# Orders of blocks 0 and 1 in a fused MLP with per-sample experts: x of block 2, the drain of block 0, and the loads of x of block 0

## The chip, the core and the metric

The kernel runs on one core of a Trainium2 chip. The metric is the device time of one execution in microseconds (us); the time of a kernel is the median of its runs.

## The reference

```python
def ref(x, indices, fc1_w, fc1_b, fc2_w, fc2_b, experts_w, experts_b):
    h = gelu(einsum('bnd,hd->bnh', x, fc1_w) + fc1_b)            # exact gelu
    shared = einsum('bnh,sh->bns', h, fc2_w) + fc2_b
    expert_x = einsum('bnh,bph->bnp', h, experts_w[indices]) + experts_b[indices][:, None, :]
    return concatenate([shared, expert_x], axis=-1)
out = x + ref(x, itok, fc1_w, fc1_b, fc2_w, fc2_b, experts_w, experts_b)
```

All is float32. x is 32 x 256 x 256; the hidden size is 1024; fc2_w gives 192 of the 256 outputs, and one of 16 experts, picked for each of the 32 rows of x, gives the other 64.

## The kernel before, in words

The work goes in 16 blocks (`BLOCKS`) of two rows of x, 512 tokens each. Every float32 operand of a matmul is split in a high half (rounded, by ScalarE) and a low half (the rest, by VectorE or GpSimd, which is called POOL below), and each product is made of three: high x high, high x low, low x high. fc1 of a block gives eight chunks of 128 hidden units; two chunks are a *pair*. ScalarE applies the gelu and makes the high half of a pair, then the low half is made, and `fc2_units` on TensorE (PE) multiplies pair and fc2 weights into the two accumulators of the block (`acc_ps`, one for each row of x). A *drain* on VectorE adds an accumulator to `resid`, which by then holds x plus bias (`residual` on POOL), and SyncE (SP) stores it.

Blocks 0 and 1 (`PLAIN`) make fc1 in the plain way, `conv_chunk(0)` to `conv_chunk(15)`. Blocks 2 to 15 use Strassen's scheme with seven products (`product`), which needs sums of quarters of w1 (S1 to S4, indices 0 to 3, made in the order `S_ORDER` = 0, 1, 3, 2) and of x (T1 to T4, `t_sum`). A block from 2 on is made in two groups, t = 0 for the first group of block 2. Its products stand between `fc2_units` of the block before.

Operands must lie transposed. x of block 0 and w1 are transposed by PE (`x0_bank`, `w1_bank`), everything else in two steps: a DMA brings pieces of 32 partitions, and VectorE transposes 32 x 32 squares into PSUM (`w2_square`, `experts_square`, `x_square`, `s_square`), from where ScalarE takes the high half (`..._high`) and VectorE the low half (`..._low`).

The order on each engine is written out by hand; the engines meet only at semaphores. An engine works strictly in its own order, so a step that waits holds everything behind it. What matters for the change:

- SP's queue issues the loads: x of block 0 (`load_x(0)`, one load of 512 KB, L263), the second half of w1 (L235), w2 (L286), experts 0 (L251), pieces of x of block 1 (L268), experts 1, w1's pieces for the S sums (`load_w1_pieces`, L279), pieces of x of block 2, the bias of fc2 (L294), x of block 1, and so on. The first half of w1 is issued by ScalarE's queue.
- PE starts with `warm` matmuls (L921), the transposes of x of block 0 (L915), ten more warm matmuls, the transposes of w1's first half, `first_chunk` (L954), the transposes of w1's second half, chunks 1 to 7 (L947), then `fc2_units` of block 0 between chunks 8 to 15 of block 1. Chunk c waits for the gelu of chunk c - 4. `fc2_units(0, ...)` waits for the low half of its pair, for w2 and for the experts; chunk 8 waits for `x1_low`.
- Block 2 on PE: the product with A11, then `fc2_units(1, 0)`, which waits for `plain_low(4)`, for expert half 0 of block 1 and for the drain of block 0 (`drained`, L803 to L810). The product with S1 waits for `xt_lo` (`x_sums_lo`) and for all four `s_low`.
- VectorE makes, between `x1_low` and the loop over blocks from 2 on: expert halves 0 and 1 of block 1 (L692, L700), the four S squares and lows (`s_square` L656, `s_low` L662), x of block 2 (L711, L715, L752, L757), the low halves of pairs 4 to 7 (`plain_low`, L720) and the drains of block 0 (L805, L807, L810).
- ScalarE makes the gelus (L513), the high halves of pairs (`conv_high`, L501), `s_high` (L425), `experts_high` (L441), `b_copy` (L475), `x_high` (L461, L464) and `x_sums_high` (L491).
- POOL makes the low halves of pairs 0 to 3 (L344), the four weight sums (L366), `residual(0)` (L337), `x_sums_lo` of block 2 (L352), `residual(1)`.

## Time and profile before

| | us |
|---|---|
| median of 3 runs | 374.62 (374.12 to 375.15) |
| the profiled execution | 375.64 |
| its span | 373.9 |
| PE busy in it | 360.3 (96%) |
| VectorE, ScalarE, POOL busy | 223.9 (60%), 243.2 (65%), 221.7 (59%) |
| HBM read, written | 28.97 MB, 8.39 MB |

The profile is of one execution. All times of rows are counted from the start of its span; 1.74 us of the execution lie outside of it. In the names of rows, numbers are left out: `fc_ps` is fc1_ps, `w_in` is w1_in (which also takes the S sums), `w_piece` is w1_piece or w2_piece, `b` is b1 or b1_in. "idle before" is the time in which the engine had nothing to do just before a row, with what ended it.

### The profile page before, as it was taken

Reading aid. Unit: us, or ns where it says so; the run is one execution under the profiler, and the core shown is the slowest. Engines: PE = TensorE matmul, PEld = TensorE weight load, DVE = VectorE, ACT = ScalarE, POOL = GpSimd, SP = SyncE. Lnnn points to the kernel's source line nnn. Section 1 sums busy time; section 2 is a strip of 40 time slices with the busy share of each in tenths; the row PEclk is TensorE's granted clock in tenths of the full one; section 3 lists DMA queues with packets and bytes.
Section 4 is the critical chain, followed back from the end, with each engine's and each line's share of the span. In section 5 each row is a group of like instructions: output and inputs, shape, how many; then the busy total and the mean of one; then the engine's idle time right before and its main releaser. Section 6 shows DMA issues by size and latency. Waiting matters only on the chain.

```text
span 373.9 us, 7841 instructions
## 1 busy us (share of the span) xinstructions
PE 360.3 (96%) x2863; PEld 353.4 (95%) x2863; DVE 223.9 (60%) x367; ACT 243.2 (65%) x410; POOL 221.7 (59%) x100
## 2 busy tenths in 40 slices
PE   6999939999999999999999999999999999999996
PEld 4788939999999999999999999999999999999996
DVE  1583788394765839386683938567393856744341
ACT  2495536675785957577594857769485767947560
POOL 0059440477666666766666677656667775666381
PEclk9899978999999999999999999999999999999999
DMA  8979844326160432516133252605135230403011
GB/s 193 187 156 108 160 107 120 86 68 166 41 177 27 131 94 87 149 53 161 48 113 95 89 146 64 169 30 149 57 93 142 64 114 31 125 23 114 2 56 56
DMA packets 70431, 37.86 MB, mean 101 GB/s; under 512 B 43514, under 2 KB 70394, under 8 KB 70394
## 3 DMA queue, kind: packets, MB, share of 16 engines
q1 hardware_dynamic: 69776, 36.85, 39.4%
q10 hardware_dynamic: 618, 0.53, 0.7%
q8 instruction: 22, 0.36, 0.4%
q14 instruction: 15, 0.12, 0.1%
HBM read 28.97 MB, written 8.39 MB: 100 GB/s over the span
## 4 chain that ended last, share of the span: by engine, by line
PE 81%; issue 3%; DVE 3%; ACT 2%; POOL 1%; DVEq 0%; POOLq 0%
PE fc_ps L971 36%; PE acc_ps L1003 15%; PE acc_ps L1005 15%; PE acc_ps L1007 15%; POOL ht L344 1%; ACT ht L501 1%; DVE ht L720 1%; DVE w1t L662 1%; DVE work L715 0%; ACT gelu L513 0%; ACT gelu L527 0%; DVE tr_ps L656 0%; DVE tr_ps L711 0%; DVE work L785 0%; DVE resid L810 0%
## 5 line engine op out<-in xcount | busy, mean ns | idle before, releaser
L344 POOL TENSOR_TENSOR ht<-gelu,ht 128x1024 fp32r<-128x1024 f32 x60 | 144.2, 2404 | 124.5 <-ACT ht L501 124.5
L971 PE MATMUL fc_ps<-xt,w1t 128*128 128x256 f32 x1176 | 173.9, 284 | 0.0
L971 PEld LDWEIGHTS fc_ps<-xt,w1t 128*128 128x128 f32 x1176 | 155.8, 193 | 0.6 <-ACT gelu L513 0.3
L1003 PE MATMUL acc_ps<-w2t,ht 128*128 128x256 f32 x512 | 145.8, 285 | 5.8 <-DVE resid L807 5.7
L1005 PE MATMUL acc_ps<-w2t,ht 128*128 128x256 f32 x512 | 145.5, 284 | 0.0
L1007 PE MATMUL acc_ps<-w2t,ht 128*128 128x256 f32 x512 | 145.5, 284 | 0.0
L1003 PEld LDWEIGHTS acc_ps<-w2t,ht 128*128 128x128 f32 x512 | 99.0, 193 | 6.5 <-issue 5.8
L1005 PEld LDWEIGHTS acc_ps<-w2t,ht 128*128 128x128 f32 x512 | 99.0, 193 | 0.3
L1007 PEld LDWEIGHTS acc_ps<-w2t,ht 128*128 128x128 f32 x512 | 99.0, 193 | 0.0
L501 ACT ACTIVATE ht<-gelu 128x1024 fp32r<-128x1024 f32 x64 | 67.8, 1063 | 3.3
L487 ACT ACTIVATE work<-fc_ps 128x512 f32<-128x512 f32 x28 | 16.8, 599 | 57.4 <-PE fc_ps L971 57.4
L769 DVE TENSOR_TENSOR work<-fc_ps,work 128x512 f32<-128x512 f32 x28 | 19.3, 691 | 54.6 <-PE fc_ps L971 45.8
L352 POOL TENSOR_TENSOR xt<-work,xt 128x1024 fp32r<-128x1024 f32 x14 | 33.6, 2403 | 17.9 <-ACT xt L491 17.9
L337 POOL TENSOR_TENSOR resid<-resid,bias 128x1024 f32<-128x1024 f32 x16 | 38.7, 2416 | 0.9 <-DMA bias<-in_L_cond_fc_b 0.9
L778 DVE TENSOR_TENSOR work<-fc_ps,work 128x512 f32<-128x512 f32 x28 | 19.2, 686 | 32.0 <-PE fc_ps L971 32.0
L441 ACT ACTIVATE w2t<-tr_ps 128x512 fp32r<-128x512 f32 x32 | 18.7, 590 | 29.0 <-PE acc_ps L1007 29.0
L527 ACT ACTIVATE gelu<-work,b 128x512 f32<-128x512 f32 x56 | 37.1, 712 | 0.7 <-DVE work L785 0.7
L785 DVE TENSOR_TENSOR work<-fc_ps,work 128x512 f32<-128x512 f32 x28 | 19.4, 692 | 12.9 <-PE fc_ps L971 11.2
L539 ACT ACTIVATE gelu<-work,b 128x256 f32<-128x256 f32 x56 | 25.2, 501 | 0.0
L700 DVE TENSOR_TENSOR w2t<-tr_ps,w2t 128x512 fp32r<-128x512 f32 x32 | 22.1, 692 | 4.7 <-ACT w2t L441 3.1
L793 DVE TENSOR_TENSOR work<-fc_ps,work 128x512 f32<-128x512 f32 x28 | 19.1, 684 | 7.2 <-PE fc_ps L971 7.2
L544 ACT ACTIVATE gelu<-fc_ps,b 128x256 f32<-128x256 f32 x56 | 23.2, 469 | 0.0
(57 smaller groups left out, 281.7 us busy)
## 6 DMA issues: line engine op xcount, KB each, us to landing
resid<-in_x SPq DMA_DIRECT2D x16, 512.0 KB, 4.0
pieces<-in_L_cond_experts_w SPq DMA_DIRECT2D x128, 64.0 KB, 1.9
out<-resid SPq DMA_DIRECT2D x32, 256.0 KB, 2.7
pieces<-in_x SPq DMA_DIRECT2D x60, 128.0 KB, 3.7
bias<-in_L_cond_experts_b SPq DMA_DIRECT2D x32, 32.0 KB, 2.9
w_piece<-in_L_cond_fc_w SPq DMA_DIRECT2D x4, 256.0 KB, 4.6
w_piece<-in_L_cond_fc_w SPq DMA_DIRECT2D x4, 192.0 KB, 8.1
w_in<-in_L_cond_fc_w SPq DMA_DIRECT2D x4, 128.0 KB, 5.8
```

The lines of the kernel that those rows point to most:

```text
L337: nc.gpsimd.tensor_tensor(rows, rows, bias[:, par, :, :].unsqueeze(2).to_broadcast([P, R, T, OUT]), ALU.add).then_inc(resid_ready, 1)
L344: nc.gpsimd.tensor_tensor(ht[:, slot, LO, :, :].rearrange("p k t -> p (k t)"), gelu[:, q % GELUS, :, :].rearrange("p k t -> p (k t)"), ht[ ...
L352: nc.gpsimd.tensor_tensor(xt[:, n % 2, X_T1:X_T4 + 1, LO, :], t_sum, xt[:, n % 2, X_T1:X_T4 + 1, HI, :].bitcast(FP32), ALU.subtract).then_ ...
L501: nc.scalar.activation(ht[:, q % PAIRS, HI, :, :].rearrange("p k t -> p (k t)"), gelu[:, q % GELUS, :, :].rearrange("p k t -> p (k t)"), A ...
L527: nc.scalar.activation(gelu[:, q % GELUS, j, :], upper[:, j, :], ACT.Gelu, bias=b1[:, k:k + 1]).then_inc(up_gelu, 1)
L539: nc.scalar.activation(gelu[:, q % GELUS, j, SEQ:2 * SEQ], c22[:, j, :], ACT.Gelu, bias=b1[:, k:k + 1]).then_inc(c22_gelu, 1)
L544: nc.scalar.activation(gelu[:, q % GELUS, j, 0:SEQ], fc1_ps[:, BANK_A[t % 2], j * SEQ:(j + 1) * SEQ], ACT.Gelu, bias=b1[:, k:k + 1]).then_ ...
L700: nc.vector.tensor_tensor(expert_columns(LO, ks), tr_ps[:, half, :].rearrange("p (k b c) -> p b k c", k=HALF, b=R), expert_columns(HI, ks) ...
L971: last = nc.tensor.matmul(fc1_ps[:, dst, j * SEQ:(j + 1) * SEQ], w1t[:, w, wv, ms], xt[:, n % 2, o, xv, :], start=(fresh and j == 0 and at ...
L1003: nc.tensor.matmul(dst, h_hi_t, w_hi, start=(r == 0 and u % (2 * T) == 0), stop=True, skip_group_check=True)
L1005: nc.tensor.matmul(dst, h_hi_t, w_lo, start=False, stop=True, skip_group_check=True)
L1007: last = nc.tensor.matmul(dst, h_lo_t, w_hi, start=False, stop=True, skip_group_check=True)
```

## The change

Loads of x of block 0: two loads of 256 KB, each with a semaphore of its own, in place of one; SP waits for the first of them before it issues the second half of w1 and all that follows. PE transposes each half of x when it is there. The pieces of x of block 2 are issued ahead of experts 1 and w1's pieces. VectorE and ScalarE take the second half of w1 ahead of w2. On VectorE x of block 2 goes ahead of expert half 0 of block 1 and of the S steps, the drains of block 0 go behind the last S step and ahead of `plain_low(6)`; ScalarE follows with `b_copy`, `x_high`, `x_sums_high` and the S steps; POOL makes `x_sums_lo` of block 2 ahead of the weight sums.

```diff
@@ -112,6 +112,7 @@
                     for n in range(PLAIN)]
         xt0 = xt_plain[0]
 
+        x0_loaded = [sem(f"x0_loaded{b}") for b in range(R)]
         x_loaded = [sem(f"x_loaded{n}") for n in range(2)]
         xp_loaded = [sem(f"xp_loaded{n}") for n in range(2)]
         e_loaded = [sem(f"e_loaded{n}") for n in range(2)]
@@ -280,7 +281,11 @@
                                  .rearrange("p q k j -> p (q k) j"), w1_pieces[q])\
                         .then_inc(w1p_loaded, 16)
 
-            load_x(0)
+            for b in range(R):
+                ts = slice(b * T, (b + 1) * T)
+                sp.dma_start(resid[:, 0, ts, :], x_blocks[0][:, ts, :]).then_inc(x0_loaded[b], 16)
+
+            sp.wait_ge(x0_loaded[0], 16)
             load_w1(sp, 1)
             for q in range(Q):
                 sp.dma_start(w2_piece[S * q:S * (q + 1), :, :], w2_v[q]).then_inc(w2_loaded, 16)
@@ -288,9 +293,9 @@
             numbers = load_experts(0)
             load_x_pieces(1)
             load_expert_bias(0, numbers)
+            load_x_pieces(2)
             numbers = load_experts(1)
             load_w1_pieces()
-            load_x_pieces(2)
             sp.dma_start(
                 bias[:, :, :, 0:SHARED].rearrange("p a b o -> p (a b) o"),
                 fc2_b.rearrange("(o c n) -> o c n", o=1, c=1).to_broadcast([P, 2 * R, SHARED]))\
@@ -331,7 +336,11 @@
         def _(pool):
             def residual(n):
                 par = n % 2
-                pool.wait_ge(x_loaded[par], 16 * (n // 2 + 1))
+                if n == 0:
+                    for b in range(R):
+                        pool.wait_ge(x0_loaded[b], 16)
+                else:
+                    pool.wait_ge(x_loaded[par], 16 * ((n + 1) // 2))
                 pool.wait_ge(be_loaded[par], 16 * R * (n // 2 + 1))
                 rows = resid[:, par, :, :].rearrange("p (b t) d -> p b t d", b=R)
                 nc.gpsimd.tensor_tensor(
@@ -373,6 +382,7 @@
 
             for r in range(PAIRS):
                 pair_lo(r)
+            x_sums_lo(PLAIN)
             pool.wait_ge(w1p_loaded, 16 * Q)
 
             pool.wait_ge(w1_tr, 2 * D)
@@ -386,7 +396,6 @@
 
             pool.wait_ge(x0_tr, D)
             residual(0)
-            x_sums_lo(PLAIN)
             residual(1)
             for n in range(PLAIN, BLOCKS):
                 for g in range(GROUPS):
@@ -566,9 +575,9 @@
             act.wait_ge(b1_ready, 1)
             conv_chunk(0)
             w1_high(1, 0)
+            w1_high(1, 1)
+            conv_chunk(1)
             w2_high(0)
-            conv_chunk(1)
-            w1_high(1, 1)
             w2_high(1)
             conv_chunk(2)
             w2_high(2)
@@ -585,24 +594,24 @@
                 x1_high(d)
             conv_chunk(7)
             conv_high(2)
+            b_copy(PLAIN)
+            x_high(PLAIN)
+
+            conv_chunk(8)
             conv_high(3)
-
-            conv_chunk(8)
+            x_sums_high(PLAIN)
             conv_chunk(9)
             conv_high(4)
             experts_high(1, 0)
             s_high(0)
             conv_chunk(10)
-            b_copy(PLAIN)
-            x_high(PLAIN)
             conv_chunk(11)
             conv_high(5)
+            s_high(1)
+            s_high(3)
             conv_chunk(12)
-            x_sums_high(PLAIN)
-            s_high(1)
             conv_chunk(13)
             conv_high(6)
-            s_high(3)
             s_high(2)
             conv_chunk(14)
             conv_chunk(15)
@@ -815,12 +824,12 @@
                 w1_low(0, d)
             dve.wait_ge(b1_tr, 1)
             nc.vector.tensor_copy(b1[:, :], fc1_ps[:, 3, 0:K]).then_inc(b1_ready, 1)
+            for d in range(D):
+                w1_low(1, d)
             w2_square(0)
             w2_square(1)
-            w1_low(1, 0)
             w2_low(0)
             w2_square(2)
-            w1_low(1, 1)
             w2_low(1)
             w2_square(3)
             w2_low(2)
@@ -837,33 +846,33 @@
                 x1_low(d)
 
             dve.wait_ge(x1_lo, D)
-            experts_square(1, 0)
-            s_square(0)
-            plain_low(4)
-            experts_low(1, 0)
-            s_low(0)
-            dve.wait_ge(e_lo, 3)
-            dve.wait_ge(s_lo, 1)
             for d in range(D):
                 x_square(PLAIN, d)
-            plain_low(5)
             x_sums_first(PLAIN)
             x_low(PLAIN, 0)
             x_sums_last(PLAIN)
             x_low(PLAIN, 1)
             dve.wait_ge(xb_lo, 2)
             dve.wait_ge(t_added, 4)
+            experts_square(1, 0)
+            plain_low(4)
+            s_square(0)
+            experts_low(1, 0)
+            s_low(0)
+            dve.wait_ge(e_lo, 3)
+            dve.wait_ge(s_lo, 1)
             s_square(1)
             s_square(3)
-            plain_low(6)
+            plain_low(5)
             s_low(1)
             s_low(3)
-            drain(0, 0)
-            drain(0, 1)
             dve.wait_ge(s_lo, 3)
             s_square(2)
             experts_square(1, 1)
             s_low(2)
+            drain(0, 0)
+            drain(0, 1)
+            plain_low(6)
             plain_low(7)
 
             for n in range(PLAIN, BLOCKS):
@@ -921,9 +930,14 @@
                     nc.tensor.matmul(fc1_ps[:, 2, 0:2 * P], bits[:, 0:P], bits,
                                      start=True, stop=True)
 
-            def x0_bank(d):
-                transposes(tr_ps[:, d, :], [feature_chunk(resid[:, 0, t, :], d)
-                                            for t in range(TILES)]).then_inc(x0_tr, 1)
+            def x0_banks(b):
+                pe.wait_ge(x0_loaded[b], 16)
+                for d in range(D):
+                    last = transposes(tr_ps[:, d, b * SEQ:(b + 1) * SEQ],
+                                      [feature_chunk(resid[:, 0, b * T + t, :], d)
+                                       for t in range(T)])
+                    if b == R - 1:
+                        last.then_inc(x0_tr, 1)
 
             def w1_bank(half, d):
                 transposes((acc_ps, tr_ps)[half][:, d, :], [
@@ -1013,9 +1027,8 @@
 
             pe.wait_ge(ident_ready, 1)
             warm(WARM)
-            pe.wait_ge(x_loaded[0], 16)
-            for d in range(D):
-                x0_bank(d)
+            for b in range(R):
+                x0_banks(b)
             warm(WARM // 2)
             pe.wait_ge(w1_loaded[0], 16 * Q)
             for d in range(D):
```

VectorE, from the squares of x of block 2 or the S squares up to `plain_low(7)` and what follows it. First the kernel before (L656 is `s_square`, L662 `s_low`, L720 `plain_low`, L805 to L810 the drains, L692 an expert square):

```order
L656 STREAM_TRANSPOSE tr_ps<-w1_in 128x512 x2
L720 TENSOR_TENSOR ht<-gelu,ht 128x1024
L662 TENSOR_TENSOR w1t<-tr_ps,w1t 128x512 x2
L805 TENSOR_TENSOR resid<-acc_ps,resid 128x2x192
L807 TENSOR_TENSOR resid<-acc_ps,resid 128x2x64
L810 TENSOR_TENSOR resid<-acc_ps,resid 128x512
L656 STREAM_TRANSPOSE tr_ps<-w1_in 128x512
L692 STREAM_TRANSPOSE tr_ps<-pieces 128x4x4x32
L662 TENSOR_TENSOR w1t<-tr_ps,w1t 128x512
L720 TENSOR_TENSOR ht<-gelu,ht 128x1024
```

The changed kernel at the same place (L665 is `s_square`, L671 `s_low`, L729 `plain_low`, L814 to L819 the drains):

```order
L665 STREAM_TRANSPOSE tr_ps<-w1_in 128x512 x2
L729 TENSOR_TENSOR ht<-gelu,ht 128x1024
L671 TENSOR_TENSOR w1t<-tr_ps,w1t 128x512 x2
L665 STREAM_TRANSPOSE tr_ps<-w1_in 128x512
L701 STREAM_TRANSPOSE tr_ps<-pieces 128x4x4x32
L671 TENSOR_TENSOR w1t<-tr_ps,w1t 128x512
L814 TENSOR_TENSOR resid<-acc_ps,resid 128x2x192
L816 TENSOR_TENSOR resid<-acc_ps,resid 128x2x64
L819 TENSOR_TENSOR resid<-acc_ps,resid 128x512
L729 TENSOR_TENSOR ht<-gelu,ht 128x1024 x2
```

The low half of a pair between the squares and the lows was `plain_low(6)` and is `plain_low(5)` now; pair 6 stands behind the drains, which have moved behind the fourth S step.

ScalarE, from the gelu of chunk 7 on. Before (L513 is a gelu, L501 `conv_high`, L441 `experts_high`, L425 `s_high`, L475, L461 and L464 `b_copy` and `x_high` of block 2):

```order
L513 ACTIVATE gelu<-fc1_ps,b1 128x512
L501 ACTIVATE ht<-gelu 128x1024 x2
L513 ACTIVATE gelu<-fc1_ps,b1 128x512 x2
L501 ACTIVATE ht<-gelu 128x1024
L441 ACTIVATE w2t<-tr_ps 128x2x4x64
L425 ACTIVATE w1t<-tr_ps 128x512
L513 ACTIVATE gelu<-fc1_ps,b1 128x512
L475 ACTIVATE b_rows<-tr_ps 128x512
L461 ACTIVATE xt<-tr_ps 128x256
L464 ACTIVATE xt<-tr_ps 128x2x256
```

Changed (each of these lines stands nine further down, L500 is `x_sums_high`):

```order
L522 ACTIVATE gelu<-fc1_ps,b1 128x512
L510 ACTIVATE ht<-gelu 128x1024
L484 ACTIVATE b_rows<-tr_ps 128x512
L470 ACTIVATE xt<-tr_ps 128x256
L473 ACTIVATE xt<-tr_ps 128x2x256
L522 ACTIVATE gelu<-fc1_ps,b1 128x512
L510 ACTIVATE ht<-gelu 128x1024
L500 ACTIVATE xt<-work 128x4x256
L522 ACTIVATE gelu<-fc1_ps,b1 128x512
L510 ACTIVATE ht<-gelu 128x1024
L450 ACTIVATE w2t<-tr_ps 128x2x4x64
L434 ACTIVATE w1t<-tr_ps 128x512
```

x of block 2 has moved from behind chunk 10 to ahead of chunk 8, its sums ahead of chunk 9, and `conv_high(3)` stands behind the gelu of chunk 8.

POOL, before (L344 is `pair_lo`, L366 a weight sum, L337 `residual`, L352 `x_sums_lo`):

```order
L344 TENSOR_TENSOR ht<-gelu,ht 128x1024 x4
L366 TENSOR_TENSOR w1_in<-w1_piece 128x512
L366 TENSOR_TENSOR w1_in<-w1_in,w1_piece 128x512
L366 TENSOR_TENSOR w1_in<-w1_piece,w1_in 128x512
L366 TENSOR_TENSOR w1_in<-w1_piece 128x512
L337 TENSOR_TENSOR resid<-resid,bias 128x1024
L352 TENSOR_TENSOR xt<-work,xt 128x4x256
L337 TENSOR_TENSOR resid<-resid,bias 128x1024
```

and changed:

```order
L353 TENSOR_TENSOR ht<-gelu,ht 128x1024 x4
L361 TENSOR_TENSOR xt<-work,xt 128x4x256
L375 TENSOR_TENSOR w1_in<-w1_piece 128x512
L375 TENSOR_TENSOR w1_in<-w1_in,w1_piece 128x512
L375 TENSOR_TENSOR w1_in<-w1_piece,w1_in 128x512
L375 TENSOR_TENSOR w1_in<-w1_piece 128x512
L346 TENSOR_TENSOR resid<-resid,bias 128x1024 x2
```

`x_sums_lo` of block 2 has moved from between the residuals to ahead of the weight sums.

## Rows read from the trace of the kernel before

**Rows 1.** The page's slices of the span, 40 equal slices, tenths busy

```profile
PE   6999939999999999999999999999999999999996
```

**Rows 2.** TensorE's waits over the whole span: us in total, times, longest

```profile
PE acc_ps L1003 <- DVE resid L807: 5.7, 1, 5.7
PE acc_ps L915 <- DMA w_in<-in_L_cond_fc_w: 2.7, 1, 2.7
```

**Rows 3.** Windows: their us, each engine's busy us, PEclk, DMA share, GB/s

```profile
7.32:10.07 2.75, 0.01 (x1) 0.00 (x0) 0.46 (x1) 0.00 (x0) 0.00 (x0) 1.00 1.12 211
...
11.24:14.65 3.41, 3.40 (x10) 2.62 (x10) 2.37 (x5) 0.82 (x3) 0.00 (x0) 0.50 1.17 230
...
48.31:53.98 5.67, 0.00 (x0) 0.03 (x1) 5.26 (x6) 0.86 (x2) 2.58 (x2) 0.84 0.48 102
53.98:59.02 5.04, 5.01 (x22) 4.72 (x23) 3.41 (x5) 3.78 (x6) 0.00 (x0) 0.50 0.25 80
...
62.40:370.00 307.60, 307.43 (x2561) 307.06 (x2560) 186.57 (x312) 209.29 (x356) 198.34 (x83) 1.00 0.33 92
```

**Rows 4.** Timeline of VectorE: start us, us, what [idle before]

```profile
13.64 1.05 DVE L673 STREAM_TRANSPOSE acc_ps<-w_piece 128x384 f32<-128x384 f32 x2 [0.80 <-DMA w_piece<-in_L_cond_fc_w]
...
25.85 1.29 DVE L728 TENSOR_TENSOR xt<-tr_ps,xt 128x512 fp32r<-128x512 f32 x2 [0.44 <-ACT xt L455]
...
48.72 3.26 DVE L720 TENSOR_TENSOR ht<-gelu,ht 128x1024 fp32r<-128x1024 f32 x1 [1.75 <-ACT ht L501]
...
53.10 0.54 DVE L805 TENSOR_TENSOR resid<-acc_ps,resid 128x384 f32<-128x384 f32 x1
53.56 0.28 DVE L807 TENSOR_TENSOR resid<-acc_ps,resid 128x128 f32<-128x128 f32 x1
...
57.98 1.23 DVE L720 TENSOR_TENSOR ht<-gelu,ht 128x1024 fp32r<-128x1024 f32 x1 [1.56 <-ACT ht L501]
```

**Rows 5.** Timeline of TensorE, 0 to 30 us

```profile
1.53 3.75 PE L921 MATMUL fc_ps<-ident 128*128 128x256 bf16 x20 [1.53 <-POOL ident L370]
...
6.07 1.25 PE L921 MATMUL fc_ps<-ident 128*128 128x256 bf16 x10
...
11.51 2.93 PE L954 MATMUL fc_ps<-xt,w1t 128*128 128x512 f32 x6
...
27.77 1.55 PE L947 MATMUL fc_ps<-xt,w1t 128*128 128x512 f32 x6
```

**Rows 6.** Timeline of SyncE's queue, 0 to 35 us

```profile
1.24 1.92 SPq L235 DMA_DIRECT2D w_in<-in_L_cond_fc_w  x4
...
10.85 3.13 SPq L268 DMA_DIRECT2D pieces<-in_x  x4
```

**Rows 7.** Timeline of ScalarE and its queue, 0 to 30 us

```profile
1.30 1.81 ACTq L235 DMA_DIRECT2D w_in<-in_L_cond_fc_w  x4
...
21.56 0.69 ACT L513 ACTIVATE gelu<-fc_ps,b 128x512 f32<-128x512 f32 x1
```

**Rows 8.** The tile w1_in, its loads

```profile
DMA to landing us min/median/max: 3.9/5.7/7.6
```

**Rows 9.** Grouped rows of VectorE, then ScalarE, 20 to 60 us: busy us, mean ns

```profile
L711 DVE STREAM_TRANSPOSE tr_ps<-pieces 128x512 f32<-128x512 f32 x5 | 3.4, 709 | 0.2
...
L513 ACT ACTIVATE gelu<-fc_ps,b 128x512 f32<-128x512 f32 x13 | 9.0, 698 | 2.9 <-PE fc_ps L947 2.9
L501 ACT ACTIVATE ht<-gelu 128x1024 fp32r<-128x1024 f32 x8 | 8.5, 1082 | 0.1
```

**Rows 10.** The page's DMA issues: count, KB each, median us to landing

```profile
w_piece<-in_L_cond_fc_w SPq DMA_DIRECT2D x4, 256.0 KB, 4.6
```

**Rows 11.** Timeline of POOL, 20 to 75 us

```profile
33.74 1.32 POOL L366 TENSOR_TENSOR w_in<-w_in,w_piece 128x512 f32<-128x512 f32 x1
...
39.73 2.41 POOL L337 TENSOR_TENSOR resid<-resid,bias 128x1024 f32<-128x1024 f32 x1 [0.92 <-DMA bias<-in_L_cond_fc_b]
...
48.55 2.35 POOL L337 TENSOR_TENSOR resid<-resid,bias 128x1024 f32<-128x1024 f32 x1
```

## The prediction

> **What bounds the kernel now.** I read the page's slices first, then PE's waits, then windows cut at those waits, then the timeline of each engine around them. The slices [rows 1] show PE at nine tenths or more nearly everywhere, with two dents. PE's list of waits [rows 2] names what ended them: 2.7 us for the first half of w1, and 5.7 us for the drain of block 0. The windows [rows 3] give exact sizes. PE does nothing from 7.32 to 10.07; from 11.24 to 14.65 it is busy at a granted clock of 0.50, the 1.2 GHz level; it stands still from 48.31 to 53.98; from 53.98 to 59.02 it works again at 0.50. In the 307.6 us behind that, PE is busy for 307.4 at full clock. So the kernel is bound by PE, and only these four stretches can be bought. Whatever PE has gained when it leaves block 1 is kept to the end, since every later row is PE work back to back. All removed, they are worth 2.75 + 3.4/2 + 5.67 + 5.04/2 = 12.6 us; that is the far end of any gain.
>
> Who holds the second dent? VectorE's rows [rows 4] show a chain without a gap: plain_low(6) (L720) takes 3.26 us from 48.72, then s_low(1) and s_low(3) (L662), then the drains at 53.10 and 53.56, and PE starts at 53.98. PE needs neither plain_low(6) nor the lows of S for the product it waits with: fc2_units(1, 0) wants only the drain of block 0, plain_low(4) and expert half 0. The drain stands behind them only by VectorE's order.
>
> **Part 1: the start.** x of block 0 goes in two loads; SP holds w1's second half and w2 until the first has landed. The x transposes gain nothing: PE is in its warm-up matmuls until 5.28 in any case and is through with the next ten at 7.32 [rows 5]. The gain is w1's first half. SP issues its four loads from 1.24 [rows 6], ScalarE its own four from 1.30 [rows 7]. Landing takes 3.9 us for the earliest and 7.6 us for the latest [rows 8], so eight loads of 128 KB land between about 5.2 and 10.3, one each 0.73 us, and PE waits until 10.07 for four of them. With ScalarE's four alone, they would all be there at 5.2 + 3 x 0.73 = 7.4, and PE, free at 7.32, would not wait: 2.7 us gained. But SP is let go when 256 KB of x are there, which I put at 3.5 to 4, and its loads then share the engines about 1.2 us later, so the last two of ScalarE's land at half the pace, at 7.4 and 8.8. Bounds 0 and 2.7; I take 8.4, nearer to the shared landing, since one load or the other may be ahead when SP's come: a gain of **1.7**. The Trainium skill, DMA: Bandwidth & Descriptors, section Issuing engines are not separate DMA queues, says that loads of either queue run on the same sixteen engines and interleave; the rows agree (eight in a row), by it alone the landing is 8.8, and 1.3 us are gained.
>
> The clock fell at 11.24, 1.2 us after PE came back from 2.75 us without work. With 1.1 us idle instead I expect it to stay up. The first chunk (L954, six matmuls) then takes not 2.93 us but about 1.85: four products at the full rate of 0.24 us, and the last two behind VectorE's two low halves of w1, 0.65 us each [rows 4]. With the transposes behind it, still at half rate, that is **1.2** (bounds 0 and 1.7: half of the 3.4). The bytes ahead of the second half of w1 are the same, so it lands near 10.3, as now, and PE wants it when the first chunk ends, at 14.4 - 2.9 = 11.5. SP's issues run some 2.4 us later at first, but part of that is given back: four pieces of x took it 3.13 us to issue, four loads of w1 1.92 [rows 6], so it now stands in front of full queues.
>
> Does the pace behind it follow? w2 still lands at 13.6 (VectorE's first square starts at 13.64 with 0.80 us idle before it, ended by that load [rows 4]). Four rounds of square, high half and low (0.55, 0.49 and 0.55, overlapping) bring ScalarE's last high half of w2 to 17.9; conv_high(0) ends at 19.0, and from gelu 4 behind it to the end of x1_low it is 5.6 us (21.56 [rows 7] to 27.14 [rows 4]), which gives 24.5. PE takes chunk 8, which waits for x1_low, at 27.8 now [rows 5], so at 24.9. So PE's 2.9 us are kept, by 0.4 us. The w1_low(1, 1) and w1_high(1, 1) steps moved ahead cost nothing: they fill the wait for w2.
>
> **Part 2: blocks 0 and 1.** Costs of a step: a square 0.71, a gelu 0.70, a high half of a pair 1.08 [rows 9]; a low half from PSUM 0.65 (two in 1.29 [rows 4]). In the new order: x_square(2) 24.5 to 25.8 (its pieces are now issued before experts 1 and w1's pieces, at about 17 to 19; w1's own, twice as large, land 4.6 us behind their issue [rows 10]); b_copy and x_high to 26.7; sums and lows of x, 2.5 us, to 29.1; experts_square to 29.8. ScalarE: gelu 8, conv_high(3) to 28.4, sums high to 29.6, gelu 9, conv_high(4) to 31.3. POOL, at 2.4 us a subtraction and 1.3 a weight sum [rows 11]: pair 3 to 30.8, x_sums_lo to 33.2.
>
> Here two engines meet. When no POOL row ran, plain_low took 1.23 us (57.98); started 0.17 us behind residual(1) it took 3.26, which is the 2.2 us that POOL still ran and 1.1 of its own [rows 4, 11]. So plain_low(4), ready at 31.3, ends at 33.2 + 1.1 = 34.3, and the weight sums run from 34.3 to 35.3, 36.7, 38.0 and 39.5. The Trainium skill, SBUF — State Buffer, section SBUF: two separate sides, says this pair of ports is an exclusive lock and not shared bandwidth; it speaks against putting a POOL step in front of plain_low(4). Were it shared evenly, 34.3 would be 33.5, and everything below 0.8 earlier.
>
> Then s_square(0) 36.1, s_high(0) 36.7, and behind it on ScalarE gelu 10, gelu 11 and conv_high(5) to 39.0. VectorE: s_low(0), s_square(1), s_square(3) to 38.8; plain_low(5) from 39.0 to 40.6, behind the last weight sum; s_low(1), s_low(3) to 41.9; s_square(2), experts_square(1, 1) to 43.3; s_low(2) 44.0; drain(0, 0), 0.54 + 0.28, done at **44.7**, drain(0, 1) 45.4. residual(0), needed before it, waits for the fc2_b load, which let it start at 39.73 [rows 11], and ends near 43.0. PE comes to the drain at 48.31 - 2.9 = **45.4**, and to the second one 1.4 us later. So the wait of 5.67 goes, with 0.7 us to spare. What is late next: plain_low(5), (6), (7) (wanted 6 us later or more), s_low(2) for the product with S1 (wanted at 48.7, ready 44.0), and VectorE's add_c11, about 50 against PE's wish at 51.9. With no idle there, the clock has no reason to fall, and the 5.04 us at half rate return 2.52. I leave 0.3 us for small waits that I did not see.
>
> **Sum.** 1.7 + 1.2 + 5.67 + 2.52 - 0.3 = 10.8 us. The profiled execution took 375.64 (span 373.9 and 1.74 around it); 375.64 - 10.8 = 364.8. The median of the runs is 1.02 below it: 374.62 - 10.8 = **363.8**.
>
> **Rivals.**
> 1. The drain is still late. It now stands behind all four S steps, each a round trip VectorE, ScalarE, VectorE, and behind POOL, whose sums start later by x_sums_lo. My chain has some twenty links, and 0.04 us too little on each eats the 0.7. For 3 us late, with the clock low for another 3.4 us (1.7 lost): 363.8 + 4.7 = 368.5; for 1 us and no fall, 364.8. For it: the length of the chain, and the port. Against: where part 1 gives less, PE comes later and the drain has more room.
> 2. The start gives nothing: SP's loads come back too early, w1 lands at 10, the clock falls as before. Then 363.8 + 2.9 = 366.7. For it: the rows show both queues sharing. Against: SP cannot issue before some x is there.
> 3. Slower. ScalarE's s_high(0) stands ahead of gelu 10 and 11, and PE's chunk 14 needs gelu 10; s_high(0) hangs on POOL's first weight sum, that on w1's pieces, which SP now issues behind the pieces of x. From weight sum 0 to the drain is 44.7 - 35.3 = 9.4 us. Slower than now needs the drain past 53.84, so that sum past 44.4, 9 us later than I have it; if it came at 46.4, the time is 374.62 + 2 = 376.6. Against: w1's pieces land 4.6 us behind their issue [rows 10], and POOL had them by 33.7 [rows 11]; 512 KB more ahead of them cost about 2.5 us at the pace of part 1.
> 4. The change does nothing, because the drain's real release is another one (fc2_pair or resid_ready): 374.6. Against: residual(0) ended at 42.14, 11 us before the drain.
>
> **Chances.** My forecast (gain of 9 to 12.6): 0.72. Rival 1 beyond 1 us: 0.14. Rival 2: 0.09. Rival 3: 0.03. Rival 4: 0.02. 0.3% of the time, 1.1 us, is about what a measurement of this kernel can tell from no change. Faster 0.95, same 0.02, slower 0.03. The low end is 374.62 - 12.6 = 362.0; the high end takes in rival 1 at its price and a little of it with part of rival 2: 369.0.
>
> **What would show it.** In the changed profile: PE's wait for w_in 1 us or less and ended near 8.4; the clock at 1.00 from 5 to 60; no wait of PE for L814 or L816 over 0.5 us, drains of block 0 near 44.7; PE's first product of block 2 (L971 now) near 44.5; the weight sums from about 34; plain_low(4) of about 3 us. I am wrong if PE's wait for the drain is still over 2 us, if the clock falls a second time, or if w1's second half (the second eight transposes) is what PE then waits for.

## The result, and the profile after

| | us |
|---|---|
| kernel before | 374.83 (374.12 to 375.15, 4 runs) |
| changed kernel | 363.88 (363.34 to 364.43, 4 runs) |
| ratio | 0.971, 95% interval 0.969 to 0.9731 |
| profiled execution: before, changed | 375.64, 363.34 (spans 373.9, 361.5) |

The forecast was 363.8 with 362.0 to 369.0. Medians differ by 10.95 us, the two profiled executions by 12.3: the profiled execution of before is 0.8 us above its median, that of the changed kernel 0.5 below its own. The sum of the prediction has to be compared with the 12.3.

The page's slices of the changed kernel, and PE's list of waits in it (us in total, times, longest), beside [rows 1, 2]:

```profile
PE   8999999999999999999999999999999999999996
...
PEclk9999999999999999999999999999999999999999
```

```profile
PE fc_ps L930 <- POOL ident L379: 1.5, 1, 1.5
PE acc_ps L1017 <- POOL ht L353: 0.2, 1, 0.2
```

Both dents are gone. PE waits for the identity matrix at the start, 1.5 us as before, and then nowhere for more than 0.2 us. Windows cut where PE's work changes (their us, each engine's busy us, then granted clock, DMA share, GB/s), beside [rows 3]:

```profile
7.54:11.40 3.86, 3.81 (x26) 3.04 (x24) 2.21 (x5) 1.71 (x5) 0.00 (x0) 1.00 1.14 227
11.40:43.58 32.18, 32.18 (x188) 28.47 (x188) 27.62 (x42) 25.42 (x41) 22.29 (x11) 1.00 0.91 151
43.58:50.00 6.42, 6.42 (x55) 6.41 (x54) 6.38 (x10) 4.44 (x8) 1.08 (x1) 1.00 0.43 107
```

PE is busy in all of it, at a granted clock of 1.00, where the kernel before lost time in four stretches. TensorE's timeline, 0 to 30 us, beside [rows 5]:

```profile
1.53 4.12 PE L930 MATMUL fc_ps<-ident 128*128 128x256 bf16 x20 [1.53 <-POOL ident L379]
...
6.45 1.25 PE L930 MATMUL fc_ps<-ident 128*128 128x256 bf16 x10
7.54 1.12 PE L924 MATMUL acc_ps<-ident,w_in 128*128 128x128 f32 x8
...
8.86 1.83 PE L968 MATMUL fc_ps<-xt,w1t 128*128 128x512 f32 x6
...
23.92 1.55 PE L961 MATMUL fc_ps<-xt,w1t 128*128 128x512 f32 x6
```

PE takes w1 at 7.54, right behind the warm-up, without a wait; the first chunk (L968) lasts 1.83 us instead of 2.93; chunk 8 begins at 23.92 instead of 27.77, 3.85 us earlier. The queue of SP, and the landing of w1's loads (minimum, median, maximum), beside [rows 6, 8]:

```profile
3.76 1.76 SPq L236 DMA_DIRECT2D w_in<-in_L_cond_fc_w  x4
```

```profile
DMA to landing us min/median/max: 3.0/4.0/4.2
```

SP comes back at 3.76. No load of w1 takes more than 4.2 us, where the last took 7.6; ScalarE's last one is issued at 2.65 and so is there at 6.9.

VectorE and POOL up to the drain, beside [rows 4, 11] (start us, us, what, idle before):

```profile
13.21 1.04 DVE L682 STREAM_TRANSPOSE acc_ps<-w_piece 128x384 f32<-128x384 f32 x2
...
22.25 1.29 DVE L737 TENSOR_TENSOR xt<-tr_ps,xt 128x512 fp32r<-128x512 f32 x2 [0.44 <-ACT xt L464]
...
24.97 2.04 DVE L724 TENSOR_TENSOR work<-b_rows 128x256 f32<-128x256 f32 x1
26.93 0.41 DVE L724 TENSOR_TENSOR work<-tr_ps,b_rows 128x256 f32<-128x256 f32 x1
...
31.26 2.13 DVE L729 TENSOR_TENSOR ht<-gelu,ht 128x1024 fp32r<-128x1024 f32 x1 [1.44 <-ACT ht L510]
...
42.88 0.55 DVE L814 TENSOR_TENSOR resid<-acc_ps,resid 128x384 f32<-128x384 f32 x1
43.35 0.28 DVE L816 TENSOR_TENSOR resid<-acc_ps,resid 128x128 f32<-128x128 f32 x1
...
44.15 2.74 DVE L729 TENSOR_TENSOR ht<-gelu,ht 128x1024 fp32r<-128x1024 f32 x2
```

```profile
24.31 2.40 POOL L353 TENSOR_TENSOR ht<-gelu,ht 128x1024 fp32r<-128x1024 f32 x1 [0.67 <-ACT ht L510]
27.30 2.65 POOL L353 TENSOR_TENSOR ht<-gelu,ht 128x1024 fp32r<-128x1024 f32 x1 [0.58 <-ACT ht L510]
29.90 2.40 POOL L361 TENSOR_TENSOR xt<-work,xt 128x1024 fp32r<-128x1024 f32 x1
32.26 2.03 POOL L375 TENSOR_TENSOR w_in<-w_piece 128x512 f32<-128x512 f32 x1
...
39.29 2.64 POOL L346 TENSOR_TENSOR resid<-resid,bias 128x1024 f32<-128x1024 f32 x1 [0.73 <-DMA bias<-in_L_cond_fc_b]
42.27 2.40 POOL L346 TENSOR_TENSOR resid<-resid,bias 128x1024 f32<-128x1024 f32 x1 [0.33 <-DMA resid<-in_x]
```

VectorE begins with w2 (L682) at 13.21 without idle time, and x1_low (L737) ends at 23.54. The drain of block 0 (L814, L816) is done at 43.63. PE's first product of block 2 starts at 43.58 and takes 0.88, so PE wants the drain at about 44.5 and finds it there.

### The profile page after: what moved, and what is told of

Read it like the earlier page. It is cut to its first block, busy times and chain, and to the rows that moved or that the text cites. A ratio compares the mean times of both kernels' runs of the same rounds, so it can differ in the third digit from the quotient of the medians.

```text
span 361.5 us, 7842 instructions
## 1 busy us (share of the span) xinstructions
PE 356.4 (99%) x2863; PEld 350.3 (97%) x2863; DVE 224.0 (62%) x367; ACT 243.6 (67%) x410; POOL 222.2 (61%) x100
## 4 chain that ended last, share of the span: by engine, by line
PE 95%; issue 2%; POOL 1%; ACT 1%; DVE 0%; POOLq 0%
PE fc_ps L985 37%; PE acc_ps L1017 16%; PE acc_ps L1021 16%; PE acc_ps L1019 16%; PE fc_ps L961 6%; PE fc_ps L930 1%; POOL ht L353 1%; PE tr_ps L924 1%; PE fc_ps L968 1%; ACT ht L510 0%; ACT gelu L536 0%; DVE work L794 0%; DVE resid L819 0%; ACT w1t L430 0%; PE acc_ps L924 0%
## 5 line engine op out<-in xcount | busy, mean ns | idle before, releaser
L778 DVE TENSOR_TENSOR work<-fc_ps,work 128x512 f32<-128x512 f32 x28 | 19.4, 691 | 54.6 <-PE fc_ps L985 45.8
L794 DVE TENSOR_TENSOR work<-fc_ps,work 128x512 f32<-128x512 f32 x28 | 19.3, 691 | 12.8 <-PE fc_ps L985 11.2
```

## The experiments

Times are medians; each is compared with runs of the kernel before on the same chip (medians 375.07 to 375.20). "Mean clock" is the granted clock of TensorE over a whole run, which every run lists.

### Start alone, middle alone

**e1_start** is the kernel before with the first two parts of the diff only: two loads of x, SP's wait, w1's second half ahead of w2. Of the diff shown ahead it has these lines, and x0_banks and residual as the changed kernel has them:

```diff
-            load_x(0)
+            for b in range(R):
+                ts = slice(b * T, (b + 1) * T)
+                sp.dma_start(resid[:, 0, ts, :], x_blocks[0][:, ts, :]).then_inc(x0_loaded[b], 16)
+
+            sp.wait_ge(x0_loaded[0], 16)
...
+            w1_high(1, 1)
+            conv_chunk(1)
             w2_high(0)
-            conv_chunk(1)
-            w1_high(1, 1)
...
+            for d in range(D):
+                w1_low(1, d)
             w2_square(0)
             w2_square(1)
-            w1_low(1, 0)
             w2_low(0)
             w2_square(2)
-            w1_low(1, 1)
```

> The start part alone on the kernel before: x of block 0 in two loads, SP held until the first is there, w1's second half ahead of w2 on VectorE and ScalarE. My theory (start and middle are two separate savings): chunk 8 begins near 23.9 as in the changed kernel, 3.8 us earlier, the clock stays up in the first 20 us, and the wait for the drain stays, since VectorE's chain to the drain moves with the start: 374.8 - 3.5 = 371.3, with a wait of 5 to 7 us. Rival: the drain is held by something that the start does not move (the fc2_b load at 39.7, w1's pieces), then the wait for it grows by what the start gained, and the time is 374 to 375.

Measured: 374.15, ratio 0.9971 (0.9944 to 0.9999), a gain of somewhere between nothing and 2.1 us. The ten runs lie between 373.18 and 375.10 but for one at 370.03. The rival holds. In the profile chunk 8 begins at 23.50, as early as in the changed kernel, but PE's waits are these:

```profile
PE acc_ps L1017 <- DVE resid L816: 7.3, 1, 7.3
...
PE fc_ps L985 <- DVE xt L766: 0.7, 1, 0.7
```

The wait for the drain has grown from 5.7 to 7.3 us, with 0.7 us more for x_low in block 2. The drain came 1.7 us earlier (52.17 against 53.84), PE 4.3. What holds it is to be seen in VectorE's rows beside POOL's:

```profile
40.30 2.32 DVE L761 TENSOR_TENSOR xt<-b_rows,xt 128x256 fp32r<-128x256 f32 x1
...
47.10 3.21 DVE L729 TENSOR_TENSOR ht<-gelu,ht 128x1024 fp32r<-128x1024 f32 x1 [1.74 <-ACT ht L510]
...
51.90 0.27 DVE L816 TENSOR_TENSOR resid<-acc_ps,resid 128x128 f32<-128x128 f32 x1
```

```profile
39.94 2.39 POOL L346 TENSOR_TENSOR resid<-resid,bias 128x1024 f32<-128x1024 f32 x1 [3.90 <-DMA bias<-in_L_cond_fc_b]
...
46.88 2.35 POOL L346 TENSOR_TENSOR resid<-resid,bias 128x1024 f32<-128x1024 f32 x1
```

x_low (L761), a step of 0.41 us, takes 2.32: it ends when residual(0) ends at 42.33, and residual(0) could not start before the load of fc2_b landed. Then plain_low(6) (L729) stands 3.21 us beside residual(1).

**e2_middle** is the rest of the diff with the old start: against the changed kernel, the lines just shown with + and - exchanged.

> The middle part alone: the kernel before with x of block 2 early (pieces, VectorE, ScalarE, POOL) and the drains behind the last S step, but the start as before. My theory: PE waits 2.7 us for w1 and runs 3.4 us at half clock as before, has no wait for the drain and no second stretch at half clock: 5.67 + 2.52 = 8.2 us less, 366.6. Rival (the drain is only on time because the start brings the chain of VectorE forward): a wait of 1 to 3 us stays, 368 to 370.

Measured: 365.16, ratio 0.9753 (0.9727 to 0.978). No wait for the drain; the wait for w1 is the only one left:

```profile
PE acc_ps L915 <- DMA w_in<-in_L_cond_fc_w: 1.1, 1, 1.1
```

It is 1.1 us here and not 2.7, and the clock did not fall behind it, so chunk 8 begins at 25.69, 2.08 us earlier than in the profile of the kernel before, with the loads and the order of the start unchanged. Of its four runs three took 365.04 to 365.22 at a mean clock of 0.999 to 1.0, one 367.02 at 0.995. So the middle alone is worth 9.9 us, the start alone 0.95, and the start on top of the middle 365.16 - 363.88 = 1.3. The last is small: the intervals of the two ratios just touch (0.9727 and 0.9731), though all four runs of the changed kernel lie below the four of e2_middle.

### What the start is made of

**e3_no_hold**: the changed kernel without the line

```diff
-            sp.wait_ge(x0_loaded[0], 16)
```

> The changed kernel without SP's wait for the first half of x; the two loads and all orders stay. My theory (the hold is the whole gain of the start): w1's first half lands near 10 again, PE waits some 2.7 us, the clock falls for 3.4 us: 363.9 + 3.8 = 367.7. Rival (two loads and the new order of w1 and w2 carry part of it): 365 to 366.5, with a full wait for w1 but a faster way to chunk 8.

Measured: 364.24, ratio 0.9717 (0.9701 to 0.9734), not separable from the changed kernel's 0.971. Neither theory gave that. PE's one wait is

```profile
PE acc_ps L923 <- DMA w_in<-in_L_cond_fc_w: 0.9, 1, 0.9
```

and w1 is taken at 8.27, between the 7.54 of the changed kernel and the 9.2 to 10.1 of the profiles with one load of x. By these medians SP's wait is worth about 0.4 us, which the runs do not separate from nothing, and the clock did not come down behind a wait of 0.9 us for w1.

**e7_w2_order_back**: the changed kernel with w2's steps mixed into those of w1's second half again, on VectorE and ScalarE.

```diff
-            w1_high(1, 1)
-            conv_chunk(1)
             w2_high(0)
+            conv_chunk(1)
+            w1_high(1, 1)
...
-            for d in range(D):
-                w1_low(1, d)
             w2_square(0)
             w2_square(1)
+            w1_low(1, 0)
             w2_low(0)
             w2_square(2)
+            w1_low(1, 1)
```

> The changed kernel with the old order of w1's second half and w2 on VectorE and ScalarE (a square of w2 ahead of w1_low(1, 0) on VectorE, w2_high(0) and gelu 1 ahead of w1_high(1, 1) on ScalarE). w2 lands at 12.6 now and w1's second half is transposed by 11.6. My theory: VectorE and ScalarE then stand and wait for w2 with w1's steps behind it; PE's chunk 4 wants w1_low(1, 1) at 15.8, which comes near 16: 0 to 0.5 us more, 364.1. Rival (the order matters for the start gain): over 1 us more, 365 or above.

Measured: 364.12, ratio 0.9708 (0.9692 to 0.9724), as expected and not separable from the changed kernel. PE waits 0.7 us, until 16.17, for w1_low(1, 1); the order of the changed kernel removes this wait, and I had booked that order at nothing.

### What the middle is made of

**e4_drain_only**, the kernel before with

```diff
-            plain_low(6)
-            s_low(1)
-            s_low(3)
             drain(0, 0)
             drain(0, 1)
+            plain_low(6)
+            s_low(1)
+            s_low(3)
```

> The kernel before with only the two drains of block 0 moved ahead of plain_low(6), s_low(1) and s_low(3). The prediction said that the drain stands behind them only by VectorE's order. If that were all, PE's wait of 5.7 us and the half clock behind it would go: 374.8 - 8 = 367. My theory now: a new wait takes its place, because the gelus of chunks 14 and 15 stand on ScalarE behind s_high(2), which is still late; PE then stops in front of the second product of block 2 until about 55.8, against 56.9 now: 1 us less, 373.8, with a wait of PE for a gelu of 5 to 6 us in place of that for the drain.

Measured: 374.47, ratio 0.9988 (0.9976 to 1.0), hardly to be told from no change. The drain is done at 46.97, seven us earlier, and PE's wait moves to another place:

```profile
PE fc_ps L971 <- ACT gelu L513: 6.4, 1, 6.4
...
PE acc_ps L1003 <- DVE resid L807: 0.9, 1, 0.9
```

The chain of VectorE was late for the S steps too, and ScalarE makes the gelus of chunks 14 and 15 behind s_high(2), so PE now stops for a gelu.

**e11_x2_late_load**, the changed kernel with the pieces of x of block 2 issued as before:

```diff
-            load_x_pieces(2)
             numbers = load_experts(1)
             load_w1_pieces()
+            load_x_pieces(2)
```

> The changed kernel with the pieces of x of block 2 issued behind experts 1 and w1's pieces again; the orders on the engines stay changed. They land at 22.4 in the changed kernel and VectorE takes them at 23.6 without a wait; here they would land near 31.5, 8 us later. Theory (the early load is a condition of the whole middle part, and engines that work in order pass the lateness on): VectorE waits 7 to 8 us, ScalarE with it ahead of gelu 8, the drain is done near 50.5 to 51.5, PE waits 6 to 7 us with a stretch at half clock: 372 to 373. Rival (slack in the chain takes most of it up): 366 to 369.

Measured: 372.29 (370.48 to 373.69, 4 runs), ratio 0.994 (0.9916 to 0.9963). The time is the one expected, the waits are not: one of 6 to 7 us was forecast. In the profiled execution, the fastest of the four, VectorE waits 7.23 us for the pieces, until 31.46, and the drain is done at 51.18; PE waits twice:

```profile
43.94 4.60 PE L961 MATMUL fc_ps<-xt,w1t 128*128 128x512 f32 x12 [1.79 <-ACT gelu L522]
...
51.33 0.35 PE L1017 MATMUL acc_ps<-w2t,ht 128*128 128x256 f32 x1 [2.07 <-DVE resid L816]
```

The first is chunk 14 behind the gelu of chunk 10, which stands on ScalarE behind s_high(0). That is the wait of the prediction's third rival, at 1.8 us. The granted clock was 0.50 from 44.3 to 47.7, behind it. The other three runs are 1.0 to 3.2 us slower and have no profile, so what they waited for is not shown.

**e6_sums_lo_late**, the changed kernel with x_sums_lo of block 2 behind residual(0) on POOL.

```diff
-            x_sums_lo(PLAIN)
             pool.wait_ge(w1p_loaded, 16 * Q)
...
             residual(0)
+            x_sums_lo(PLAIN)
             residual(1)
```

> The changed kernel with x_sums_lo of block 2 back behind residual(0) on POOL. My theory: the weight sums come 2.4 us earlier, plain_low(4) meets a weight sum instead of a 2.4 us step, VectorE's chain to the drain is up to 2 us earlier, and PE does not gain, since it waits nowhere: 363.9 (between 363.3 and 364.4). residual(1) moves to about 44.5 to 47, and x_sums_lo to 42 to 44.5, still ahead of the product with S1 at 47. Rival: that product or plain_low(6) and (7) get late by the new neighbour and PE waits up to 1 us: 365.

Measured: 366.41, ratio 0.9772 (0.9755 to 0.9788): 2.5 us lost. The rival's place is right, its price too low.

```profile
43.97 5.25 DVE L729 TENSOR_TENSOR ht<-gelu,ht 128x1024 fp32r<-128x1024 f32 x2
...
51.08 0.67 DVE L778 TENSOR_TENSOR work<-fc_ps,work 128x512 f32<-128x512 f32 x1
```

```profile
42.38 2.41 POOL L361 TENSOR_TENSOR xt<-work,xt 128x1024 fp32r<-128x1024 f32 x1
44.75 3.39 POOL L346 TENSOR_TENSOR resid<-resid,bias 128x1024 f32<-128x1024 f32 x1
```

plain_low(6) and (7) together take 5.25 us instead of 2.74, one behind x_sums_lo, one behind residual(1); add_c11 (L778) comes at 51.08 instead of 48.75, and PE waits 1.4 us for it, then 0.4 for the next sum. The profile is of the fastest run, 365.65, at a mean clock of 1.0. The other three have 0.995, so they also had a stretch at half rate.

**e5_low6_first**, the changed kernel with plain_low(6) ahead of the two drains.

```diff
+            plain_low(6)
             drain(0, 0)
             drain(0, 1)
-            plain_low(6)
```

> The changed kernel with plain_low(6) ahead of the two drains. It prices the slack of the drain (drain(0, 0) done at 43.6 in the changed kernel, PE wants it at 44.5) and the ports that VectorE and POOL share. plain_low(6) would start at 42.9, while residual(1) runs on POOL from 42.3 to 44.7. If the ports are held for whole instructions it ends at 45.8, the drain is done at 46.6, and PE waits 2.1 us: 366.0. If they were shared, it ends near 45, PE waits 1.3 us: 365.2. If there is more slack than I think, no change: 363.9.

Measured: 366.78 (365.79 to 367.81), ratio 0.9784 (0.9756 to 0.9811). plain_low(6) takes 2.48 us from 43.86, until residual(1) is through and 1.1 us more, the drain is done at 47.01, and PE waits 1.72 us for it. The two runs above 367 have a mean clock of 0.994, the two below 0.999 and 1.0. The profiled one took 366.11; chunk 8 begins there at 24.89, 0.97 us later than in the profile of the changed kernel, so only some 1.8 us of its difference come from plain_low(6).

### What holds the drain in the kernel before

**e9_before_again** is the kernel before without an edit, for a second profile.

> The kernel before once more, for a second profile of it. Three profiles with the old start show PE on w1 at 9.2 to 10.1 and chunk 8 at 25.7 to 27.8, while the times of the kernel before differ by less than 0.5%. Theory: the drain of block 0 is held by a chain that PE's start does not move, so what an execution is earlier at the start it waits longer for the drain; chunk 8 would be at 25.7 to 26.5 here, the wait for the drain 6.5 to 8 us, the time 374 to 376. Rival: the first profile is typical, with chunk 8 near 27.8 and a wait of 5.7 us.

Measured: 376.09.

```profile
PE acc_ps L1003 <- DVE resid L807: 6.8, 1, 6.8
PE acc_ps L915 <- DMA w_in<-in_L_cond_fc_w: 2.0, 1, 2.0
```

PE's wait for w1 is 2.0, that for the drain 6.8; chunk 8 begins at 27.13 and the drain is done at 54.30. The wait has the size of the theory, chunk 8 and the time lie outside of what I wrote. What takes the earlier start away can be seen in this profile, and again in that of e4_drain_only, whose chain is the same up to the drain (VectorE's row, then POOL's):

```profile
40.61 3.10 DVE L720 TENSOR_TENSOR ht<-gelu,ht 128x1024 fp32r<-128x1024 f32 x1 [2.50 <-ACT ht L501]
...
40.23 2.40 POOL L337 TENSOR_TENSOR resid<-resid,bias 128x1024 f32<-128x1024 f32 x1 [2.05 <-DMA bias<-in_L_cond_fc_b]
```

```profile
40.29 2.63 DVE L715 TENSOR_TENSOR work<-b_rows 128x256 f32<-128x256 f32 x1
...
39.46 3.18 POOL L337 TENSOR_TENSOR resid<-resid,bias 128x1024 f32<-128x1024 f32 x1 [2.75 <-DMA bias<-in_L_cond_fc_b]
```

VectorE comes to plain_low(5) at 40.61 (e9) or 39.15 (e4), against 41.25 in the first profile. Each time the step that it has in hand when residual(0) runs on POOL ends behind residual(0): plain_low(5) in e9, 3.10 us instead of 1.23, and the first sum of x in e4, 2.63 instead of 0.41. In e9 the lead of 0.64 us has become a lag of 0.46 by the drain; in e4 a lead of 2.1 us has shrunk to 0.6 at the S squares.

The timed runs say the same. In the profiles a mean clock of 0.985 goes with two stretches at half rate as in [rows 3], and 0.991 (e4_drain_only) with the second alone. Of the 35 runs of before beside the experiments, 13 have 0.984 to 0.986, at a median of 375.24, and 22 have 0.989 to 0.991, at 375.03. So the first stretch costs some 0.2 us and not the 1.7 us that it takes from PE. This reading of the mean clock is not certain: six of the ten runs of e1_start also have 0.985 or 0.986, though PE did not wait for w1 in its profile.

**e10_start_pool_order** is e1_start with x_sums_lo ahead of residual(0) on POOL:

```diff
-            residual(0)
             x_sums_lo(PLAIN)
+            residual(0)
             residual(1)
```

> The start part alone with one more edit: on POOL x_sums_lo of block 2 ahead of residual(0), so that residual(0) no longer runs while VectorE makes the sums of x of block 2 (all loads and VectorE's order unchanged). In the start part alone residual(0) starts when fc2_b lands (39.9) and runs until 42.3, and x_low(2, 0), which reads and writes SBUF only, takes 2.32 us instead of 0.41. Theory (that meeting at the ports holds the chain to the drain): x_low takes 0.4, everything behind it on VectorE moves up by 1.9 us, plain_low(6) then meets residual(0) instead of residual(1); the drain is done near 50.6 instead of 52.2, and the time is 374.15 - 1.6 = 372.6 (371.8 to 373.3). Rival (the chain is held by w1's pieces, gelus or the order of VectorE alone): 374.2, or later by the drain's own wait for residual(0).

Measured: 372.38, ratio 0.9935 (0.992 to 0.995), 1.8 us less than e1_start; the two intervals overlap slightly, the time is the one expected.

```profile
40.29 0.41 DVE L761 TENSOR_TENSOR xt<-b_rows,xt 128x256 fp32r<-128x256 f32 x1
...
45.20 3.35 DVE L729 TENSOR_TENSOR ht<-gelu,ht 128x1024 fp32r<-128x1024 f32 x1 [1.75 <-ACT ht L510]
...
50.14 0.28 DVE L816 TENSOR_TENSOR resid<-acc_ps,resid 128x128 f32<-128x128 f32 x1
```

```profile
42.77 2.41 POOL L361 TENSOR_TENSOR xt<-work,xt 128x1024 fp32r<-128x1024 f32 x1 [6.73 <-ACT xt L500]
45.14 5.63 POOL L346 TENSOR_TENSOR resid<-resid,bias 128x1024 f32<-128x1024 f32 x2
```

x_low takes 0.41, the chain moves up by 1.8 us, the drain is done at 50.42 instead of 52.17, and plain_low(6) stands beside residual(0) instead of residual(1). Nothing but POOL's order changed, so the meeting with residual(0) held the chain back by 1.8 us in e1_start. PE still waits 5.3 us for the drain here, about what it waits in the kernel before.

### Towards a faster version

**e8_short_warm** has 3 instead of 10 matmuls in the second warm-up, **e12_warm12** also 12 instead of 20 in the first:

```diff
-            warm(WARM)
+            warm(12)
...
-            warm(WARM // 2)
+            warm(3)
```

> The changed kernel with 3 instead of 10 matmuls in the second warm-up, between the transposes of x and those of w1 (they compute nothing that is used). w1's first half is there at 6.9 and PE takes it at 7.5 to 7.7 only, since the warm-up still runs. My theory: PE starts on w1 0.7 us earlier and keeps it: 363.2, if the drain, whose slack is 0.8 us, still holds. Rival 1: VectorE and ScalarE do not follow (their chain from w2 on does not depend on PE) and PE waits for x1_low or the drain: 363.9. Rival 2: with fewer matmuls the clock falls in the first 15 us: 365 or more.

> The changed kernel with 12 instead of 20 matmuls in the first warm-up and 3 instead of 10 in the second. x's halves are there at 3.75 and 5.14, w1's first half at 6.9, and PE is in the warm-up until 5.3 to 6.0 now, longer where the clock rises late. Theory: PE takes w1 at 6.9 instead of 7.3 to 7.7 and keeps it, 0.4 us less than with 3 matmuls in the second warm-up alone: 362.9. Rival 1: the drain's slack is used up, 363.3 as there. Rival 2: PE stands still for parts of the first 7 us, the clock rises later or falls: 364 to 366.

Measured: 363.32 (ratio 0.9689, 0.9672 to 0.9705) and 363.26 (0.9686, 0.9673 to 0.9699). Both are 0.6 us below the changed kernel, but the intervals overlap with its 0.969 to 0.9731: a likely gain, not a shown one. The 0.4 us more of the second did not come. Its profile is of the slowest of its five runs, 364.36; the other four took 363.01 to 363.65. In it PE takes w1 at 6.93 and chunk 8 begins at 23.40, and yet:

```profile
42.67 0.56 DVE L814 TENSOR_TENSOR resid<-acc_ps,resid 128x384 f32<-128x384 f32 x1 [0.20 <-POOL resid L346]
...
43.94 4.00 DVE L729 TENSOR_TENSOR ht<-gelu,ht 128x1024 fp32r<-128x1024 f32 x2
```

```profile
40.16 2.41 POOL L346 TENSOR_TENSOR resid<-resid,bias 128x1024 f32<-128x1024 f32 x1 [2.09 <-DMA bias<-in_L_cond_fc_b]
43.32 2.41 POOL L346 TENSOR_TENSOR resid<-resid,bias 128x1024 f32<-128x1024 f32 x1 [0.75 <-DMA resid<-in_x]
```

The drain now waits for residual(0), which waits for fc2_b (2.09 us idle before 40.16), and plain_low(6) and (7) meet a later residual(1). PE waits 0.8 us for add_c11. So in this run what PE gains at its start is taken back behind the same load as in e1_start. In the profile of e8_short_warm (363.2) POOL waited 0.37 us for that load, plain_low(6) and (7) took 1.23 us each, and PE had no such wait.

## Why the prediction was right, point by point

- **PE is the bound and keeps what it has gained.** Right: in the changed profile PE waits 0.2 us behind the start. The signs that the prediction named came, but for two sizes: plain_low(4) took 2.13 us and not about 3, and the first product of block 2 began at 43.58 and not near 44.5.
- **w1 lands at 8.4, 1.7 us gained.** Too small for the profiled pair: it was there at 6.9, and PE took w1 at 7.54 instead of 10.07, 2.5 us earlier. The step that failed is "the last two of ScalarE's land at half the pace": SP came back at 3.76 as assumed, but its four loads landed behind ScalarE's four (at 7.5 to 9.1 in the trace, ScalarE's at 4.4 to 6.9). The rule of the Trainium skill (DMA: Bandwidth & Descriptors, Issuing engines are not separate DMA queues) that all queues share the engines and interleave gave 8.8 and was further off: here loads issued 1.1 us later landed later. The wait of SP is not the whole of it: without it w1 was taken at 8.27 (e3_no_hold).
- **Clock and first chunk, 1.2.** Right: 1.83 us against 1.85, clock at 1.00; with the transposes behind it 1.35 us. The terms named for the 1.85 (four products of 0.24, two low halves of 0.65) add up to 2.26; they overlap, since VectorE makes the low halves from 8.84 on, beside the first four products.
- **The start is worth 2.9 us on the path.** Too small for the profiled pair, where chunk 8 is 3.85 us earlier (2.5 and 1.35). It counts in full only once the chain to the drain is repaired: the profile of e2_middle has chunk 8 1.77 us later than that of the changed kernel and took 1.70 us longer. On the kernel before it gives 0.95 us alone (e1_start), since PE there waits for the end of VectorE's chain, which residual(0) holds. In the medians it is worth 1.3 on top of the middle, less than half of the 2.9: I took the start of one execution for that of all, and the old start varies (w1 taken at 9.19 to 10.07, chunk 8 at 25.67 to 27.77 in four profiles).
- **The middle is worth 5.67 + 2.52 - 0.3 = 7.9 us.** Too small: 9.9 by the medians (e2_middle). Between the profiled executions it is 10.6 us, of which 2.1 are the better start that this execution of e2_middle had, and 8.5 are left. The kernel before loses a good start in the wait for the drain; once the drain is no longer late, the executions with a good start show it. That is why the medians put more on the middle and less on the start than the sum did.
- **"The drain stands behind them only by VectorE's order."** True and misleading: moved alone it gives about 0.6 us, hardly clear of nothing (e4_drain_only), since PE then waits 6.4 us for a gelu, behind s_high(2). The saving is the whole chain brought forward, on three engines and in SP's queue (e11_x2_late_load, e6_sums_lo_late).
- **Times of the chain.** plain_low(4) 34.3, drain 44.7 against PE's wish at 45.4; measured 33.39, 43.63 and 44.5. The slack of 0.7 us was 0.8. In the chain two errors nearly cancel. VectorE did not have to wait for w2, and x1_low ended at 23.54 and not at 24.5. But the first sum of x (L724, two SBUF inputs) was held as well, 2.04 us beside pair 2's low half instead of 0.41, so x's sums ended at 29.06, where I had 29.1, and plain_low(4) started at 31.26, where I had 31.3. POOL alone kept the lead: x_sums_lo ended at 32.30 and not at 33.2, and with it plain_low(4), the first weight sum (34.29, not 35.3) and the drain came 0.9 to 1.1 us earlier.
- **The ports as a lock.** Right. plain_low(4) took 2.13 us from 31.26, which is POOL's rest until 32.30 and 1.09 more.
- **Rival 1** (the drain is still late) did not occur, but its room is 0.8 us: with one step more on VectorE the median is 2.9 us higher (e5_low6_first). **Rival 3** did not occur; its wait appears in e11_x2_late_load at 1.8 us. **Rival 2** did not occur either. Its case, w1 late and the clock down, is in none of the profiles with the drain repaired; the one run of e2_middle with a mean clock of 0.995 took 367.02, where I gave 366.7. **Rival 4** is out: PE's wait for the drain went when VectorE's chain was early (e2_middle), and residual(0) ended at 41.93, before the drain.
- **The sum.** 10.8 against 12.3 in the profiled pair and 10.95 in the medians. With the 3.85 us of chunk 8 and without the 0.3 for small waits the sum would have been 12.04. That the median was hit to 0.1 us is partly luck: the start was undersized by 1 us in the profiled pair, and the profiled executions lie on the far sides of their medians by 1.3 us in all.

What stays open: how much of the start's 1.3 us belongs to the two loads of x and how much to SP's wait; e3_no_hold and the changed kernel can't be told apart, nor can e7_w2_order_back. No profile shows where the slower runs of e5_low6_first, e6_sums_lo_late and e11_x2_late_load, and the runs of e1_start at 0.986, lost their clock. That fc2_b's load holds the next version was read in one slow execution of e12_warm12 and not tried by moving that load.

## What to carry to other kernels

What is gained ahead of an idle stretch of the bound engine counts in full only if the chain of other engines that ends this stretch moves too: otherwise it becomes a longer wait there. So first find where that chain is anchored (here a load, then a POOL step that blocks the ports), repair it, and only then count what lies ahead of it. And when a late step is moved, move what stands with it in the chain: the drain alone gave about 0.6 us, the chain 9.9. And profile the kernel before more than once when its start varies: a single execution had a wait for w1 of 2.7 us, others 0.7 to 2.0.

## What the runs showed of the hardware that I had not expected

A step with one input in PSUM was not held: s_low(1) and s_low(3) took 1.28 us for two beside residual(0). The Trainium skill, SBUF — State Buffer, section SBUF: two separate sides, says the same of steps with two SBUF inputs, and the rows agree.
- The windows show a granted clock of 1.00 from the span's start, but the first record of it in the traces stands at 4.3 to 7.4 us. The first 20 warm-up matmuls, from 1.5 us on, took 3.70 to 4.45 us, and the ten of the second warm-up 1.25. That the clock was low until then is read from these durations. After a wait of 2.0 or 2.7 us for w1 the granted clock fell to 0.50 (e9_before_again, before), after 0.7 to 1.1 us it did not (e4_drain_only, e3_no_hold, e2_middle). Behind a wait of 1.79 us it fell (e11_x2_late_load), behind one of 1.72 it did not (e5_low6_first).
- The load of fc2_b, a row written to all partitions, 384 KB, took 11.2 us from issue to landing in the kernel before and 12.0 in the changed one, where the 256 KB loads of w1's pieces took 4.6 and 4.5 us.
